# Expert weights kept on chip and addressed by a register, with the up products in split f16

## The chip, the cores and the metric

The kernel runs on one core of one Trainium2 chip. The metric is device time in microseconds of one launch. TensorE is called PE, ScalarE ACT, VectorE DVE, GpSimd POOL and SyncE SP.

## What is computed

32 images of 128 x 128 and 32 texts of 128 x 128 give 32 sequences of 192 tokens with 128 features. The part around the change is the last layer, cut here to what matters (xf is the normed sequence, K = 2 and 8 experts, F = 512):

```python
logits = xf @ router_w
gate_vals, idx = jax.lax.top_k(logits, K)
gates = jax.nn.softmax(gate_vals, axis=-1)
for e in range(E):
    h = jax.nn.relu(xf @ w1[e] + b1[e]) @ w2[e] + b2[e]
    y = _layernorm(xf + h, gamma[e], beta[e])
    w = jnp.sum(jnp.where(idx == e, gates, 0.0), axis=-1)
    out = out + w[:, None] * y
```

Ahead of it stand a noisy linear layer with a gate for the 64 patches of each image, the joining with the text, a norm, attention with 8 heads, a residual and a norm with weights, and one more norm. All is float32; the kernel already forms keys and queries from f16 halves.

## The kernel before

The work of every engine is written out by hand as one list of calls, with semaphores between engines.

**Attention stage.** The 32 sequences go in 16 pairs of 384 columns. PE embeds, forms keys, queries and values, scores (L828, L855), weighted values (L870, L873) and the projection. ACT copies and exponentiates (L599, L609, L633), DVE takes row maxima and norms, POOL shifts and scales rows (`shifted` L1616, `scale1` L1604 to L1610, which waits for DVE). DVE picks two experts for each token, and POOL sends each token's row to `sorted_d` in DRAM, to the place of its expert, by indirect DMA (`send`, L1653). SP issues nearly all loads. Among them is `pack(e)` (L442 to L450), which for each of the eight experts copies w1 and w2 (256 KB each), the small first bias, and gamma, beta and b2 (64 KB each, repeated over 128 rows) from their inputs into one DRAM tensor `pack_d`, six DMAs for each expert.

**Expert stage.** The sorted rows form 56 tiles: 47 of 256 rows and 9 of 128. A small `plan` on chip tells the expert of each tile. For a tile g SP does two things: `load(g)` (L475 to L483) reads the 256 token rows into `xs`, and `load_weights(g)` (L486 to L496) reads the expert from the plan into a register with `value_load` (L487), waits until the slot is free, and loads one expert's whole pack, 1413 floats a partition, into one of six slots `ws`. Four slots lie in the buffer of the stacked keys and queries (`stk`), two in one half of the exponentials' buffer (`pexs`).

PE works in steps (`step_b(nxt, cur, old)`, L933 to L966): the transposes of tile t+1 (L943), the up products of tile t (L953: four f32 matmuls with 256 columns, two records each in the trace), the down products of tile t-1 (L965: eight f32 matmuls with 128 columns, sixteen records). A tile of 128 rows has 128 columns in the up products, one transpose and half the down products. ACT's step (L663 to L681) copies the turned rows to SBUF (L668), makes four Relu passes (L675) and a square root (L681). DVE (L1418 to L1472) adds residual, bias and up result, norms, and gives the place of each row; POOL scatters the two halves of each result to `expert_d` (L1667). `b_xs`, `b_up`, `b_hid`, `b_dn` and `b_y` are the semaphores of turned rows, up products, hidden rows, down products and finished rows.

**Tail.** SP reads the results back (L530), ACT weights them (L722), DVE adds them (L1543, L1548), and SP stores them (L539, L542).

The lists of the stages overlap: PE's first ten expert steps stand among the last pieces of attention and routing of pairs 13 to 15.

## Time and profile before

| What | Value |
|---|---|
| Median of three runs | 606.3 us (605.55 to 612.3) |
| The profiled execution | 610.3 us |
| Its span from the first to the last instruction | 608.6 us |
| Mean granted TensorE clock | 0.936 of full speed |
| Moved by DMA | 101.61 MB, 167 GB/s on average |

The profiled execution is 1.7 us longer than its span and 4.0 us over the median. PE is the matmuls and PEld the weight loads, which overlap them; "issue" is idle time for which the profile shows no releaser, "remote" one that it puts down to no engine of the trace. Register operations are not counted as busy. Lines are those of the code above.

### The profile page before, as it was taken

Reading aid. Unit: us, or ns where it says so; the run is one execution under the profiler, and the core shown is the slowest. Engines: PE = TensorE matmul, PEld = TensorE weight load, DVE = VectorE, ACT = ScalarE, POOL = GpSimd, SP = SyncE. Lnnn points to the kernel's source line nnn. Section 1 sums busy time; section 2 is a strip of 40 time slices with the busy share of each in tenths; the row PEclk is TensorE's granted clock in tenths of the full one; section 3 lists DMA queues with packets and bytes.
Section 4 is the critical chain, followed back from the end, with each engine's and each line's share of the span. In section 5 each row is a group of like instructions: output and inputs, shape, how many; then the busy total and the mean of one; then the engine's idle time right before and its main releaser. Section 6 shows DMA issues by size and latency. Waiting matters only on the chain.

```text
span 608.6 us, 15887 instructions
## 1 busy us (share of the span) xinstructions
PE 505.8 (83%) x4764; PEld 402.4 (66%) x4764; DVE 445.2 (73%) x1768; ACT 343.2 (56%) x793; POOL 307.1 (50%) x447
## 2 busy tenths in 40 slices
PE   4899999988998799977667998798878998989800
PEld 3776676656666566755445797697767988989700
DVE  5875788966776589767656488478667778777797
ACT  4575667756566466755444555455354554655662
POOL 2530224577644645746726578555555555345430
PEclk9999999998999889989968999698999999999965
DMA  5266644361434216333103736566678989888599
GB/s 161 80 195 167 161 123 117 89 180 33 150 115 112 75 61 145 98 98 104 45 15 126 260 106 215 173 182 220 198 216 248 285 267 288 257 285 262 168 340 258
DMA packets 75078, 101.61 MB, mean 167 GB/s; under 512 B 10750, under 2 KB 58785, under 8 KB 74994
## 3 DMA queue, kind: packets, MB, share of 16 engines
q1 hardware_dynamic: 54114, 77.61, 43.4%
q0 software_dynamic: 6416, 12.93, 6.1%
q10 hardware_dynamic: 14464, 10.06, 5.5%
q8 instruction: 39, 0.64, 0.5%
q14 instruction: 45, 0.37, 0.2%
HBM read 74.40 MB, written 32.38 MB: 175 GB/s over the span
## 4 chain that ended last, share of the span: by engine, by line
PE 32%; issue 21%; DVE 15%; POOL 11%; another core or an unknown queue 6%; SPq 6%; ACT 5%; DMA 2%; ACTq 1%; POOLq 0%; DVEq 0%
PE sbk L953 7%; POOL sorted_d L1653 6%; PE avb L965 3%; PE mbk L965 3%; PE mbk L828 2%; PE avb L768 2%; PE sbk L855 2%; PE avb L870 2%; PE avb L873 1%; PE gen L768 1%; DVE pexs L1455 1%; DVE stat L1461 1%; POOL rs L1639 1%; PE gen L776 1%
## 5 line engine op out<-in xcount | busy, mean ns | idle before, releaser
L1156 DVE TENSOR_REDUCE mx<-mbk 128x4 f32<-128x768 f32 x96 | 91.1, 949 | 49.3 <-PE mbk L828 31.3
L1653 POOL DMA_INDIRECT sorted_d<-pay,slot x96 | 96.1, 1001 | 41.4 <-issue 26.5
L1667 POOL DMA_INDIRECT expert_d<-pexs,dest x70 | 70.4, 1006 | 65.0 <-DVE pexs L1455 46.1
L633 ACT ACTIVATE pexs<-sbk 128x768 f32<-128x768 f32 x96 | 77.5, 808 | 37.1 <-PE sbk L855 29.0
L953 PE MATMUL sbk<-pexs,stk 128*128 128x256 f32 (+1 forms) x304 | 71.4, 379 | 6.3 <-issue 4.4
L675 ACT ACTIVATE pexs<-sbk,stk 128x256 f32<-128x256 f32 (+1 forms) x152 | 59.5, 456 | 20.0 <-PE sbk L953 10.3
L953 PEld LDWEIGHTS sbk<-pexs,stk 128*128 128x128 f32 x304 | 54.1, 198 | 14.2 <-issue 8.3
L1667 POOL DMA_INDIRECT expert_d<-xT,dest x33 | 32.8, 995 | 34.2 <-DVE xT L1455 19.0
L668 ACT ACTIVATE pexs<-mbk 128x256 f32<-128x256 f32 (+1 forms) x55 | 19.7, 359 | 49.2 <-remote 38.5
L828 PE MATMUL mbk<-stk 48*64 48x192 f16 (+1 forms) x512 | 34.2, 258 | 14.8 <-DVE mx L1156 11.2
L855 PE MATMUL sbk<-stk 49*64 49x192 f16 (+1 forms) x512 | 34.8, 260 | 9.8 <-ACT pexs L633 5.7
L1616 POOL TENSOR_TENSOR kept<-h,lnb 128x384 f32<-128x384 f32 x16 | 16.0, 1000 | 50.9 <-DVE h L1131 50.7
L768 PE MATMUL avb<-ident 128*128 128x128 f32 x246 | 37.8, 296 | 0.0
L965 PEld LDWEIGHTS mbk<-stk,pexs 128*128 128x128 f32 x272 | 35.2, 200 | 2.5 <-issue 1.5
L965 PE MATMUL mbk<-stk,pexs 128*128 128x128 f32 x272 | 35.4, 283 | 1.4 <-issue 1.4
L870 PE MATMUL avb<-pexs,vxs 128*32 128x192 f32 x512 | 35.6, 352 | 0.5 <-issue 0.4
L873 PE MATMUL avb<-pexs,vxs 128*32 128x192 f32 x512 | 35.4, 342 | 0.6 <-issue 0.6
L965 PE MATMUL avb<-stk,pexs 128*128 128x128 f32 x288 | 35.3, 275 | 0.0
L768 PEld LDWEIGHTS avb<-ident 128*128 128x128 f32 x246 | 32.4, 201 | 4.4 <-issue 2.0
L965 PEld LDWEIGHTS avb<-stk,pexs 128*128 128x128 f32 x288 | 34.8, 192 | 0.8
L828 PEld LDWEIGHTS mbk<-stk 48*64 48x64 f16 (+1 forms) x512 | 12.3, 101 | 34.6 <-DVE mx L1156 17.2
L953 PE MATMUL sbk<-pexs 128*128 128x256 f32 (+1 forms) x144 | 31.8, 364 | 2.8 <-ACT pexs L675 2.8
(255 smaller groups left out, 1203.6 us busy)
## 6 DMA issues: line engine op xcount, KB each, us to landing
stk<-pack_d SPq DMA_DIRECT2D x38, 706.5 KB
pexs<-pack_d SPq DMA_DIRECT2D x18, 706.5 KB
stack_d<-kq ACTq DMA_DIRECT2D x48, 192.0 KB
stk<-stack_d SPq DMA_DIRECT2D x64, 144.0 KB
xn<-sorted_d SPq DMA_DIRECT2D x47, 132.0 KB
pack_d<-in_w SPq DMA_DIRECT2D x16, 256.0 KB
xin<-in_xp SPq DMA_DIRECT2D x16, 128.0 KB, 3.8
h<-in_txt SPq DMA_DIRECT2D x16, 128.0 KB, 3.6
```

Source lines behind the costliest of these rows:

```text
L633: act.activation(pex[p % 2][m][:, :, :], sbk[:, :, 0:COLS], ACT.Exp, scale=0.25).then_inc(a_pex, 1)
L675: act.activation(hid[cur % 2][:, c, 0:n], bank[4 + c // 2][:, (c % 2) * G:(c % 2) * G + n], ACT.Relu, bias=ws[cur % 6][:, AT_B1 + c:AT_B1 ...
L768: pe.matmul(place[:, COLS:512], ident[:, :], ident[:, :], start=True, stop=True)
L828: last = pe.matmul(dst, queries, keys, start=True, stop=True)
L855: last = pe.matmul(dst, keys, queries, start=True, stop=True)
L870: pe.matmul(dst, v[:, 1 + b, head, :], e[3 * g + 2 * pair][:, half, b * SEQ:(b + 1) * SEQ], start=True, stop=False)
L873: last = pe.matmul(dst, v[:, 3 * b, head, :], e[3 * g + 1][:, half, pair * SEQ:(pair + 1) * SEQ], start=False, stop=True)
L953: last = pe.matmul(bank[4 + c // 2][:, (c % 2) * G:(c % 2) * G + n], ws[cur % 6][:, c * P:(c + 1) * P], xsT[cur % 2][:, 0:n], start=True, ...
L965: last = pe.matmul(ok, hid[old % 2][:, c, k * P:(k + 1) * P], ws[old % 6][:, F + c * D:F + (c + 1) * D], start=(c == 0), stop=(c == FC - 1))
L1156: dve.tensor_reduce(dst, mbk[:, :, 0:COLS].rearrange("p h (c s) -> p h c s", c=2), AX.X, ALU.max).then_inc(d_mx, 1)
L1653: pool.indirect_dma_start(sorted_d[:, :], bass.IndirectOffsetOnAxis(ap=slot[p % 6][:, 2 * k + w:2 * k + w + 1], axis=0), pay[p % 6][:, k, ...
L1667: pool.indirect_dma_start(expert_d[:, :], bass.IndirectOffsetOnAxis(ap=dest[fin % DESTS][:, k:k + 1], axis=0), ye[fin % RESULTS][:, k, :], ...
```

## The change

The numbers for which only part of a tile's pack is loaded fall to 389 floats a partition (first bias, an id, gamma, beta and b2), and all six slots lie in one buffer. `pack(e)` loses its copies of w1 and w2 and has four DMAs.

w1 of all experts (2 MB) comes by one DMA early in the attention stage. It is split: POOL multiplies it by 256 (`enlarge`), ACT rounds it to f16 (`high_weights`), POOL subtracts that from it and rounds the rest to f16 (`low_weights`), each eight times with 128 x 512 elements. w2 of all experts (2 MB) comes as f32 by three DMAs (`second_weights`) into the key and query buffer, when the last score products of pairs 12 to 14 are done.

In an expert step PE reads the tile's expert into a register (`which`). The rows are turned two steps ahead; ACT makes the high half in f16 (`high`), PE takes it off the turned rows in PSUM by one f16 matmul with -1/256 times the identity (`drop_high`), and ACT makes the low half (`low`). The up products are, for each of four chunks, three f16 matmuls (high by high, low by high, high by low), whose weights are addressed by the register. The Relu pass scales by 1/65536. The down products stay eight f32 matmuls, with w2's rows addressed by the register. SP and POOL have the same calls per tile as before, save for waits.

Beside this, buffers of the plan and of the tail lie in other memory (`spare` goes, the second and third group of results lie in `hs`, `kqs`, `flat0`), semaphores of the setup are merged, and POOL fills one more 128 x 128 constant, `less`, at the start.

The core of the diff:

```diff
-AT_B1 = F + FC * D
+AT_B1 = 0
 AT_ID = AT_B1 + FC
 AT_LN = AT_ID + 1
-WROW = F + FC * D + FC + 1 + 3 * D
+WROW = FC + 1 + 3 * D
+SPLIT = 256.0
...
-        ws = [stk32[:, i * (4 * COLS):i * (4 * COLS) + WROW] for i in range(4)] + [flat0[:, i * WROW:(i + 1) * WROW] for i in range(2)]
+        ws = [flat0[:, i * WROW:(i + 1) * WROW] for i in range(6)]
+        w1s = sb("w1s", [P, NE, 2, F], F16)
+        w1f = flat1[:, 0:NE * F].rearrange("p (e f) -> p e f", e=NE)
+        w2s = stk32[:, 0:NE * FC * D].rearrange("p (e c d) -> p e c d", e=NE, c=FC)
...
-        xsT = [room(2048 + 256 * i, (G,)) for i in range(2)]
+        xsT = [room(2048 + 256 * i, (G,)).bitcast(F16).rearrange("p (a t) -> p a t", a=2) for i in range(2)]
...
-        spare = sb("spare", [P, 2 * GROUP * TILES * D])
-        y1 = [group_of(stk32, 3072), group_of(vxf, 0), group_of(spare, 0), group_of(stk32, 0)]
-        y2 = [group_of(stk32, 4608), group_of(vxf, 1536), group_of(spare, 1536), group_of(stk32, 1536)]
-        w_in, wa_in, small_made = sem("w_in"), sem("wa_in"), sem("small_made")
+        hsf = hs[:, :, :, :].rearrange("p i t d -> p (i t d)")
+        kqf = kqs[:, :, :, :].rearrange("p i j t -> p (i j t)").bitcast(F32)
+        assert 6 * WROW <= 2560
+        y1 = [group_of(stk32, 4608), group_of(vxf, 0), group_of(hsf, 0), group_of(stk32, 0)]
+        y2 = [group_of(flat0, 2560), group_of(vxf, 1536), group_of(kqf, 0), group_of(stk32, 1536)]
...
             def pack(e):
-                sp.wait_ge(small_made, 1)
-                for at, src in ((0, a["w1"][e]), (AT_B1, small[:, e, :]), (AT_LN, a["gamma"][e:e + 1, :].to_broadcast([P, D])),
+                sp.wait_ge(setup, 3)
+                for at, src in ((AT_B1, small[:, e, :]), (AT_LN, a["gamma"][e:e + 1, :].to_broadcast([P, D])),
                                 (AT_LN + D, a["beta"][e:e + 1, :].to_broadcast([P, D])),
                                 (AT_LN + 2 * D, a["b2"][e:e + 1, :].to_broadcast([P, D]))):
                     sp.dma_start(pack_d[e, :, at:at + src.shape[1]], src).then_inc(pack_out, 16)
-                sp.dma_start(pack_d[e, :, F:F + FC * D].rearrange("p (c d) -> p c d", c=FC),
-                             a["w2"][e].rearrange("(c p) d -> p c d", p=P)).then_inc(pack_out, 16)
-            PACKS = 6 * NE
+            PACKS = 4 * NE
+            def first_weights():
+                sp.dma_start(w1f, a["w1"].rearrange("e p f -> p e f")).then_inc(w12_in, 16)
+            def second_weights(i):
+                after(sp, pe_s, PAIRS - 4 + i, MERGED)
+                lo, hi = 3 * i, min(3 * i + 3, NE)
+                sp.dma_start(w2s[:, lo:hi, :, :].rearrange("p e c d -> p (e c) d"),
+                             a["w2"][lo:hi].rearrange("e (c p) d -> p (e c) d", p=P)).then_inc(w12_in, 16)
...
+            ldx(0); ldt(0); load_weights_a(); ldx(1); ldt(1); ldx(2); ldt(2); ldx(3); ldt(3); ldx(4); ldt(4); first_weights(); ldx(5)
...
             def load_weights(g):
                 e = sp.value_load(plan[0:1, 1, slot_of(g):slot_of(g) + 1], min_val=0, max_val=NE - 1)
-                if g < 4:
-                    after(sp, pe_s, PAIRS - 4 + g, MERGED)
-                elif g < 6:
+                if g < 6:
                     after(sp, pe_av, PAIRS - 2, 2)
                 after(sp, b_y, g - 6)
-                after(sp, b_dn, g - 6)
                 sp.dma_start(ws[g % 6], pack_d[bass.ds(e, 1), :, :].rearrange("a p f -> (a p) f")).then_inc(ws_in[g % 6], 16)
-            load_weights(0)
-            load_weights(1)
+            second_weights(0)
+            second_weights(1)
             for p in range(EARLY_PAIRS - 6, EARLY_PAIRS):
                 after_dma(sp, sent, p, 6)
             load(0)
             load(1)
+            second_weights(2)
+            load_weights(0)
+            load_weights(1)
             for g in range(2, 6):
...
+            def high_weights(e):
+                act.wait_ge(w1_made, e + 1)
+                act.activation(w1s[:, e, 0, :], w1f[:, e, :], ACT.Copy).then_inc(act_fills, 1)
...
+                if p == 1 and m == 0:
+                    act.wait_ge(w1_made, 2 * NE)
...
-            def step_b(nxt, cur):
-                if 0 <= nxt < GRID:
-                    act.wait_ge(b_xt, nxt + 1)
-                    after(act, b_up, nxt - 2, 2)
-                    n = chunks(nxt) * P
-                    act.activation(xsT[nxt % 2][:, 0:n], (bank[6] if nxt else gen_of("b0", 0))[:, 0:n], ACT.Copy).then_inc(b_xs, 1)
-                if 0 <= cur < GRID:
-                    n = chunks(cur) * P
+            def turned(t):
+                return (bank[6] if t else gen_of("b0", 0))[:, 0:chunks(t) * P]
+            def high(t):
+                if t < GRID:
+                    act.wait_ge(b_xt, t + 1)
+                    after(act, b_up, t - 2, 2)
+                    act.activation(xsT[t % 2][:, 0, 0:chunks(t) * P], turned(t), ACT.Copy, scale=SPLIT).then_inc(b_hi, 1)
+            def low(t):
+                if t < GRID:
+                    act.wait_ge(b_ng, t + 1)
+                    act.activation(xsT[t % 2][:, 1, 0:chunks(t) * P], turned(t), ACT.Copy, scale=SPLIT).then_inc(b_xs, 1)
+            def hidden(t):
+                if t < GRID:
+                    n = chunks(t) * P
                     for c in range(FC):
-                        act.wait_ge(b_up, cur * 2 + c // 2 + 1)
+                        act.wait_ge(b_up, t * 2 + c // 2 + 1)
                         if c == 0:
-                            after(act, b_dn, cur - 2)
-                        act.activation(hid[cur % 2][:, c, 0:n], bank[4 + c // 2][:, (c % 2) * G:(c % 2) * G + n],
-                                       ACT.Relu, bias=ws[cur % 6][:, AT_B1 + c:AT_B1 + c + 1]).then_inc(b_hid, 1)
-                if ROOT <= cur - 2 < GRID:
-                    old = cur - 2
-                    after(act, b_rs, old - 2)
-                    act.wait_ge(b_mv, old + 1)
-                    act.activation(sd4[old % 2][:, 0:chunks(old)], mv4[old % 2][:, 0:chunks(old), 1], ACT.Sqrt, bias=epsf[:, 0:1]).then_inc(b_sd, 1)
+                            after(act, b_dn, t - 2)
+                            after_dma(act, ws_in, t)
+                        act.activation(hid[t % 2][:, c, 0:n], bank[4 + c // 2][:, (c % 2) * G:(c % 2) * G + n], ACT.Relu,
+                                       bias=ws[t % 6][:, AT_B1 + c:AT_B1 + c + 1], scale=1.0 / (SPLIT * SPLIT)).then_inc(b_hid, 1)
+            def root(t):
+                if ROOT <= t < GRID:
+                    after(act, b_rs, t - 2)
+                    act.wait_ge(b_mv, t + 1)
+                    act.activation(sd4[t % 2][:, 0:chunks(t)], mv4[t % 2][:, 0:chunks(t), 1], ACT.Sqrt, bias=epsf[:, 0:1]).then_inc(b_sd, 1)
+            def step_b(t):
+                low(t + 1)
+                hidden(t)
+                high(t + 2)
+                root(t - 2)
...
+            xt(3); high_weights(0); high_weights(1); hi(3); vcopy(2); vcopy(3); high_weights(2); lo(3); xt(4); xnorm(5); hi(4); mxt(0); xt(5); gexp(6); lo(4); gexp(7)
+            high_weights(3); high_weights(4); hi(5); high_weights(5); lo(5); soft(0, 0); soft(0, 1); soft(0, 2); soft(0, 3); high_weights(6); high_weights(7); context(0, 0); soft(0, 4); soft(0, 5)
...
-            def step_b(nxt, cur, old):
-                if 0 <= nxt < GRID:
-                    after_dma(pe, xs_in, nxt)
-                    if nxt == 0:
+            expert = {}
+            def which(t):
+                if t < GRID:
+                    pe.wait_ge(plan_made, 1 if t < EARLY else 3)
+                    expert[t] = pe.value_load(plan[0:1, 1, slot_of(t):slot_of(t) + 1], min_val=0, max_val=NE - 1)
+            def turned(t):
+                return bank[6] if t else gen_of("b0", 0)
+            def turn(t):
+                if t < GRID:
+                    after_dma(pe, xs_in, t)
+                    if t == 0:
                         freed(gen_at, "b0", 0)
-                    if nxt == 1:
+                    if t == 1:
                         after(pe, d_cn, PAIRS - 1)
-                    after(pe, b_xs, nxt - 1)
-                    turned = bank[6] if nxt else gen_of("b0", 0)
-                    for k in range(chunks(nxt)):
-                        last = pe.transpose(turned[:, k * P:(k + 1) * P], xs[nxt % 6][:, k, 0:D], ident[:, :])
+                    after(pe, b_xs, t - 1)
+                    for k in range(chunks(t)):
+                        last = pe.matmul(turned(t)[:, k * P:(k + 1) * P], xs[t % 6][:, k, 0:D], ident[:, :], start=(k == 0), stop=True,
+                                         is_transpose=True, skip_group_check=True)
                     last.then_inc(b_xt, 1)
-                if 0 <= cur < GRID:
-                    after_dma(pe, ws_in, cur)
-                    pe.wait_ge(b_xs, cur + 1)
-                    if cur == 0:
-                        after(pe, a_pex, PAIRS - 1, MERGED)
-                    n = chunks(cur) * P
+            def drop_high(t):
+                if t < GRID:
+                    n = chunks(t) * P
+                    pe.wait_ge(b_hi, t + 1)
+                    pe.matmul(turned(t)[:, 0:n], less[:, :], xsT[t % 2][:, 0, 0:n], start=False, stop=True,
+                              skip_group_check=True).then_inc(b_ng, 1)
+            def up(t):
+                if t < GRID:
+                    n = chunks(t) * P
                     for c in range(FC):
-                        after(pe, b_hid, cur - 1, FC, c + 2 - c % 2)
-                        last = pe.matmul(bank[4 + c // 2][:, (c % 2) * G:(c % 2) * G + n],
-                                         ws[cur % 6][:, c * P:(c + 1) * P], xsT[cur % 2][:, 0:n], start=True, stop=True)
+                        if c == 0:
+                            pe.wait_ge(b_xs, t + 1)
+                        after(pe, b_hid, t - 1, FC, c + 2 - c % 2)
+                        if t == 0 and c == 0:
+                            pe.wait_ge(w1_made, 2 * NE)
+                            after(pe, a_pex, PAIRS - 1, MERGED)
+                        for i, (x, w) in enumerate(((0, 0), (1, 0), (0, 1))):
+                            rows = w1s[:, bass.ds(expert[t], 1), w, c * P:(c + 1) * P].rearrange("p e f -> p (e f)")
+                            last = pe.matmul(bank[4 + c // 2][:, (c % 2) * G:(c % 2) * G + n], rows, xsT[t % 2][:, x, 0:n],
+                                             start=(i == 0), stop=(i == 2))
                         if c % 2:
                             last.then_inc(b_up, 1)
-                if 0 <= old < GRID:
-                    if old == 0:
+            def down(t):
+                if 0 <= t < GRID:
+                    pe.wait_ge(b_hid, t * FC + FC)
+                    after(pe, b_z, t - 2)
+                    if t == 0:
+                        pe.wait_ge(w12_in, 16 * 4)
                         after(pe, a_cx, PAIRS - 1, 2)
-                    pe.wait_ge(b_hid, old * FC + FC)
-                    after(pe, b_z, old - 2)
-                    for k in range(chunks(old)):
-                        ok = bank[3 + 4 * (old % 2)][:, k * D:(k + 1) * D]
+                    for k in range(chunks(t)):
+                        ok = bank[3 + 4 * (t % 2)][:, k * D:(k + 1) * D]
                         for c in range(FC):
-                            last = pe.matmul(ok, hid[old % 2][:, c, k * P:(k + 1) * P],
-                                             ws[old % 6][:, F + c * D:F + (c + 1) * D], start=(c == 0), stop=(c == FC - 1))
+                            rows = w2s[:, bass.ds(expert[t], 1), c, :].rearrange("p e d -> p (e d)")
+                            last = pe.matmul(ok, hid[t % 2][:, c, k * P:(k + 1) * P], rows, start=(c == 0), stop=(c == FC - 1))
                     last.then_inc(b_dn, 1)
+            def step_b(t):
+                drop_high(t + 1)
+                up(t)
+                which(t + 1)
+                turn(t + 2)
+                down(t - 1)
...
+            which(0); turn(0); turn_x2(13); drop_high(0); turn_context(15); up(0); which(1); route(13); turn_c(15)
+            turn(1); down(0); project(15); drop_high(1); count(13); turn(2); drop_high(2); up(1); which(2); turn(3)
+            step_b(2); turn_x2(14); step_b(3); route(14); step_b(4); count(14); step_b(5); step_b(6); step_b(7)
+            turn_x2(15); step_b(8); route(15); step_b(9); count(15)
...
+            def enlarge(e):
+                if e == 0:
+                    pool.wait_ge(w12_in, 16)
+                pool.tensor_scalar(w1f[:, e, :], w1f[:, e, :], SPLIT, None, ALU.mult).then_inc(w1_made, 1)
+            def low_weights(e):
+                pool.wait_ge(act_fills, 4 + e + 1)
+                pool.wait_ge(w1_made, e + 1)
+                pool.tensor_tensor(w1s[:, e, 1, :], w1f[:, e, :], w1s[:, e, 0, :], ALU.subtract).then_inc(w1_made, 1)
...
+            scale1(1); shifted(2); scale1(2); shifted(3); scale1(3); shifted(4); scale1(4); enlarge(0); enlarge(1); enlarge(2); shifted(5); scale1(5)
+            enlarge(3); enlarge(4); enlarge(5); enlarge(6); enlarge(7); low_weights(0); low_weights(1); low_weights(2)
+            low_weights(3); low_weights(4); low_weights(5); shifted(6); scale1(6); low_weights(6); low_weights(7); shifted(7); scale1(7); shifted(8); scale1(8); shifted(9); scale1(9); scale2(0)
```

## Rows read from the trace of the kernel before

**Rows 1.** the page: busy time of the engines, and the chain that ended last

```profile
PE 505.8 (83%) x4764; PEld 402.4 (66%) x4764; DVE 445.2 (73%) x1768; ACT 343.2 (56%) x793; POOL 307.1 (50%) x447
...
PE 32%; issue 21%; DVE 15%; POOL 11%; another core or an unknown queue 6%; SPq 6%; ACT 5%; DMA 2%; ACTq 1%; POOLq 0%; DVEq 0%
```

**Rows 2.** windows, core 0: us, busy and count by engine, granted clock, DMA share, GB/s

```profile
250.00:345.40 95.40, 74.56 (x909) 51.95 (x908) 59.10 (x248) 49.43 (x96) 55.09 (x77) 0.89 0.31 93
345.40:578.60 233.20, 208.87 (x1432) 192.84 (x1430) 174.06 (x802) 123.62 (x347) 126.25 (x134) 0.97 0.73 228
578.60:608.60 30.00, 0.14 (x2) 0.00 (x0) 25.60 (x84) 14.27 (x47) 6.06 (x6) 0.55 0.93 299
```

**Rows 3.** timeline of PE, full tiles: start us, us, engine, line, operation, tiles, count

```profile
370.00 1.89 PE L953 MATMUL sbk<-pexs,stk 128*128 128x256 f32 x8
371.73 1.95 PE L965 MATMUL mbk<-pexs 128*128 128x128 f32 x16
373.51 0.38 PE L943 MATMUL mbk<-ident,xn 128*128 128x128 f32 x2
373.73 0.60 PE L953 MATMUL sbk<-pexs,stk 128*128 128x256 f32 x2
```

**Rows 4.** the same view, a half tile and a full one in turn

```profile
486.38 1.06 PE L953 MATMUL sbk<-pexs,stk 128*128 128x128 f32 x8
...
492.00 1.89 PE L953 MATMUL sbk<-pexs,stk 128*128 128x256 f32 x8
```

**Rows 5.** waits of the expert stage (total us, times, longest us), one stall of PE

```profile
ACT pexs L668 <- remote: 38.5, 12, 5.2
...
PEld mbk L943 <- DMA xn<-sorted_d: 5.4, 4, 2.5
...
383.05 1.50 PE L953 MATMUL sbk<-pexs,stk 128*128 128x256 f32 x4 [3.81 <-issue]
```

**Rows 6.** timeline of PE: f16 matmuls of 384 columns, and three small bf16 ones

```profile
78.15 0.49 PE L801 MATMUL sbk<-kq,minus 128*128 128x384 f16 x2
...
352.81 0.17 PE L929 MATMUL gen<-oh,before 128*128 128x24 bf16 x1
352.84 0.22 PE L924 MATMUL gen<-oh,onesb 128*128 128x16 bf16 x3
```

**Rows 7.** chain of waits at 461 us, SyncE: start us, us, what (plan read, address, move, DMA)

```profile
461.10 0.26 SPq L487
...
461.71 0.04 SPq L496
...
461.80 0.03 SPq L496
...
461.86 0.34 SPq L496
```

**Rows 8.** timeline of DVE, one round of tiles; groups of the stage by line

```profile
370.94 0.61 DVE L1425 SCALAR_TENSOR_TENSOR pexs<-pexs,mv,stk 128x128 f32<-128x128 f32 x2
...
373.90 0.35 DVE L1425 SCALAR_TENSOR_TENSOR pexs<-pexs,mv 128x128 f32<-128x128 f32 x1
...
L1667 POOL DMA_INDIRECT expert_d<-pexs,dest x66 | 66.4, 1006 | 61.5 <-DVE pexs L1455 44.2 <-issue 16.5 <-DVE dest L1436 0.6
...
L675 ACT ACTIVATE pexs<-sbk,stk 128x256 f32<-128x256 f32 x128 | 52.5, 472 | 17.0 <-PE sbk L953 7.5 <-remote 5.5 <-issue 3.4
```

**Rows 9.** DMA issues of the page: tensors, queue, operation, count, KB each

```profile
stk<-pack_d SPq DMA_DIRECT2D x38, 706.5 KB
...
pack_d<-in_w SPq DMA_DIRECT2D x16, 256.0 KB
```

**Rows 10.** attention stage: windows row, one POOL wait, and line L599

```profile
47.40:97.00 49.60, 48.00 (x552) 32.68 (x549) 36.76 (x82) 31.59 (x60) 9.16 (x20) 1.00 0.57 148
...
64.18 1.00 POOL L1616 TENSOR_TENSOR kept<-h,lnb 128x384 f32<-128x384 f32 x1 [16.74 <-DVE h L1131]
...
L599 ACT ACTIVATE kq<-sbk x16: 788/810/811, 26.6 to 279.4; 128x768 f16<-128x768 f32 x16
```

85 lines of the change are left out of this document (42 added, 43 removed).

## The prediction, made before the changed kernel had run

> **What bounds the kernel now.** I read the page first. TensorE is the busiest engine (505.8 us, 83% of a 608.6 us span) and the largest named share of the chain that ended last, 32%, but "issue", DVE and POOL share the rest [rows 1], so the stages have to be read one by one. The windows say that up to 345.4 us the attention stage runs, then 233.2 us of expert tiles in which PE is busy 208.87 us, DVE 174.06, ACT 123.62 and POOL 126.25 at a DMA share of 0.73, and that in the last 30 us PE does nothing and DMA is 0.93 busy [rows 2]. The change works in the middle one, and in the attention stage it adds work.
>
> Inside an expert step the PE timeline shows what is paid. A full tile (256 rows) starts 3.73 us after the one before (370.00 to 373.73): two transposes, eight up records in 1.73 us (370.00 to 371.73), sixteen down records in 1.78 (371.73 to 373.51) and 0.22 for the next transposes, with no gap [rows 3]. A half tile and a full one together take 5.62 us (486.38 to 492.00) [rows 4]. With 47 full and 9 half tiles, 38 lone full ones and 9 such pairs make 38 x 3.73 + 9 x 5.62 = 192 us of the 233; the other 41 are the attention leftovers, slow starts and stalls. The waits list names them: ACT's copy of the turned rows waits 38.5 us for "remote", PEld waits 5.4 us for row loads; and before 383.05 us one tile stands for 3.81 us in "issue" [rows 5]. What a stall is worth is thus not known from its name, but the array is the limit of every clean tile.
>
> **The up products.** One f32 matmul of 256 columns (two records) becomes three f16 ones. The f16 pair L801 has 384 columns: two in 0.49 us. The small bf16 ones of 16 to 24 columns show 0.17 us from start to end with hardly any streaming, so 0.49 - 0.17 = 0.32 us is the streaming of two, 0.16 each; 256 columns are 0.107 us. Twelve of them: 1.29 us for 1.73. One more, drop_high, 0.107; transposes 0.22 and down 1.78 as they are. Array time of a full tile: 0.22 + 0.11 + 1.29 + 1.78 = 3.40, say 3.43 with the joints; 0.30 saved. A pair of half and full: 0.33 + 0.16 + 1.94 + 2.67 = 5.1 for 5.62 [rows 3, 4, 6].
>
> **The register.** This is the unknown. PE now reads the tile's expert from the plan and its 12 up weights and 8 down rows are addressed by it. No row shows a TensorE instruction like that. The nearest are SyncE's, which does the same for each weight load. On the chain at 461 us: the plan read starts at 461.10, the address computation at 461.71, a move at 461.80, the DMA at 461.86 [rows 7]. So a read costs 0.61 us, one address 0.09 (0.04 of it the operation), a move 0.06. Plain instructions cost the PE sequencer next to nothing: three bf16 matmuls with weights in 0.22 us where one takes 0.17, 0.03 apart [rows 6]. Sequencer time of a full tile: 0.61 + 20 x (0.09 + 0.03) + 11 other pairs x 0.03 = 3.3 us, just under the array's 3.43: hidden, if the sequencer can run ahead. For a half tile: 0.61 + 16 x 0.12 + 6 x 0.03 = 2.7; a pair of half and full is 6.0, over the array's 5.1 and over the 5.62 of before. The lower end is nothing (address computed beside the array, 3.43); the upper has all 28 addressed records (the 16 down records one by one) at address, move and issue, 0.18: 0.61 + 5.0 = 5.7 us a tile. I take the 0.12, because a matmul needs the address and no descriptor, and 20, one for each matmul written. The Trainium skill (TensorE: Matmul & The Clock Gate, "Wait — 56ns, not 53.3ns?") says that a MATMUL decoded by the sequencer's own code costs about 62 ns. The 0.03 spacing shows that plain ones here don't pay it; whether addressed ones do, no row shows; by that rule the full tile would be 3.3 + 20 x 0.062 = 4.5 us, estimated from that page.
>
> Stage: 38 x (3.43 - 3.73) = -11.4; 9 pairs x (6.0 - 5.62) = +3.4, of which the sequencer's lead from full tiles (0.13 each) takes half: +1.7. Sum -9.7.
>
> **The other engines in a step.** They must fit below 3.43. DVE's chain repeats from 370.94 to 373.90, 2.96 us [rows 8]: it fits by 0.5. ACT: four Relus and now two copies of the same size for one, at most 6 x 0.472 = 2.8 us, and a small square root. POOL has two scatters of 1.006 us and idles 16.5 us of the stage before 66 of them for their issue, 0.25 each: 2.5 us a tile. In the early tiles sends of the same kind come on top, which makes some of these tiles POOL's [rows 8]. Transposes are issued two steps ahead and ACT halves them in two passes with a PE pass between (low waits for drop_high); its place at the step's head gives it a step of cover. If it is late, each tile pays a pass, 0.47 us.
>
> **Loads.** The per-tile load falls from 706.5 KB to 199 [rows 9]: 56 x 0.507 = 28.4 MB less, in a stage of 228 GB/s [rows 2]. PE was no longer waiting for weights but for rows [rows 5]; these 5.4 us stand behind the same queue. About half of it goes: -3. It could be all the stalls in part (-12) or none.
>
> **The attention stage.** DVE leads POOL there: POOL waits 16.74 us at 64.18 for h, and is busy 9.16 us of the 49.6 from 47.4 on [rows 10]. The eight enlargements and eight subtractions, 128x512, by the tensor operation of 128x384 at 1.0 us are at most 1.33 each: 21 us. They fill the 16.7 us window and spill 4 to 5 into those behind, all with idle time: 0, at worst one pair late by 5. ACT gets 8 copies, 0.5 to 0.8 each by the 0.81 of 768 columns [rows 10]: 5 us in a stretch in which it is busy 31.59 of 49.6 and PE 48.0; the score chain waits at times for ACT, so I charge half, +2.5. Soft(1,0) waits for the last halves; behind it stand the whole score rows of pair 1. The 2 MB load, 7 us at the tail's 299 GB/s [rows 2], stands ahead of the inputs of pairs 5 and later, which are loaded many pairs ahead. Against this 16 DMA to DMA copies of 256 KB, 8 MB in and out, and their issues on SP are gone [rows 9]; SP only feeds buffers there: -0.5. Sum +2, ends -1 and +8. The second weights (three loads, 2 MB) come at the end of that stage, at a DMA share of 0.31 [rows 2], ahead of row loads 0 and 1 on SP: +1. The tail reads the same bytes: 0.
>
> **Sum.** -9.7 - 3 + 2 + 1 = -9.7 us against the profiled execution, which took 610.3 (span 608.6 and 1.7 around it), 4.0 above the median of 606.3. So 596.5 on the scale of the medians. About 1%, 6 us, is what a measurement of this kernel can tell from no change.
>
> **Rivals.**
> (A) The sequencer becomes the bound. Every matmul with a register costs more than (3.73 - 0.61 - 0.33)/20 = 0.14 us: from there on the expert step is slower than before. At address, move and issue (0.18, 20 times) a full tile is 4.5 and a half one 3.7: 38 x 0.8 + 9 x 2.6 = +54, so 660; with 28 addressed records at 0.12 it is 4.1 and 3.1: 38 x 0.33 + 9 x 1.5 = +26, so 630. I take 635. For it: SP's rows. Against it: the read and the addresses need nothing of the tile before, and can run while the array works. The 4.5 us by the Trainium skill's figure for sequencer decoding falls at its upper end.
> (B) PE's time is not the limit on average. 41 us of stage don't come from the array, and a faster one waits longer for DVE, POOL's scatters and the freezes. Then only part of the 9.7 comes, and the attention stage's additions eat it: 604. For it: "remote" and "issue" waits that no PE row explains. Against it: runs of clean tiles at 3.73.
> (C) The loads were behind the stalls. With 28 MB less, SP's queue and the row loads are on time and a third of the 41 us goes: -14 beside the 9.7: 583. For it: the step of 378 us. Against it: "remote" stalls lie also where the DMA share is low.
>
> **Chances.** Forecast 0.35 (596.5, own range 590 to 601); A 0.28; B 0.17; C 0.17; that the early splitting delays pair 1 by more than 8 us 0.03. Range 578 to 640: it leaves out the upper half of A. Faster by over 1% (under 600.2): 0.28 + 0.17 + 0.02 = 0.47; within 1%: 0.07 + 0.15 = 0.22; slower: 0.31.
>
> **What would show it.** Full tiles starting 3.4 us apart in the PE timeline, up 1.3 of it; no "issue" gaps between the addressed matmuls. A: up records 0.13 or more apart instead of 0.107, down pairs over 0.112, PE waiting for its own queue. B: 3.4 us bursts and larger waits of ACT and DVE. C: fewer "remote" waits. DMA share of the stage near 0.4; the first expert tile at 345 to 349 us, later if the splitting hurts. The prediction is wrong if a clean full tile takes over 3.6 us.

## The result, and the profile after

The changed kernel takes 641.17 us in the median (640.78 to 644.29, four runs) against 605.92 for the kernel before, a ratio of 1.0615 with a 95% interval of 1.0553 to 1.0677. It is slower by some 35 us. The forecast was 596.5 us, the range ended at 640, and rival A, on the slower side, was priced at 635. The profiled execution has a span of 639.1 us. Some executions of a kernel run slower than its others at a lower granted clock; the ratios leave these out, and no stage times are given from them.

The page of the changed kernel, its busy times and the chain that ended last:

```profile
PE 508.0 (79%) x5044; PEld 393.1 (62%) x5044; DVE 448.5 (70%) x1768; ACT 360.8 (56%) x857; POOL 329.2 (52%) x465
...
PE 46%; ACT 15%; another core or an unknown queue 11%; issue 10%; DVE 8%; DMA 4%; ACTq 2%; SPq 2%; POOL 1%; DVEq 0%; POOLq 0%
```

Beside [rows 1], ACT has grown from 5% to 15% of the chain, with only 17.6 us more work. The windows of the changed kernel (columns as in [rows 2]) say where the time went:

```profile
250.00:346.10 96.10, 80.50 (x939) 55.17 (x939) 62.63 (x259) 52.10 (x102) 58.62 (x83) 0.89 0.33 94
346.10:607.70 261.60, 210.45 (x1710) 183.77 (x1709) 176.14 (x802) 136.26 (x401) 126.07 (x133) 0.94 0.36 100
607.70:639.10 31.40, 0.00 (x0) 0.00 (x0) 26.00 (x84) 15.03 (x49) 6.25 (x6) 0.53 0.93 297
```

The first up product starts at 346.10 us, where it started at 345.39: the split of w1 on POOL and ACT and the early load cost the attention stage 0.7 us. The tail is 1.4 us longer. The expert stage grew from 233.2 to 261.6 us, 28.4 of the 30.5 us, although its DMA share fell from 0.73 to 0.36 and its rate from 228 to 100 GB/s.

A clean tile is what was forecast. The timeline of PE (columns as in [rows 3]):

```profile
493.57 1.47 PE L1024 MATMUL sbk<-pexs,w1s 128*128 128x256 f16 x12
494.88 0.38 PE L999 MATMUL mbk<-ident,xn 128*128 128x128 f32 x2
495.10 1.98 PE L1041 MATMUL avb<-stk,pexs 128*128 x16
496.92 0.27 PE L1008 MATMUL mbk<-pexs,less 128*128 128x256 f16 x1
497.03 1.47 PE L1024 MATMUL sbk<-pexs,w1s 128*128 128x256 f16 x12
498.42 0.30 PE L999 MATMUL mbk<-ident,xn 128*128 128x128 f32 x1
```

The timeline of ACT in the same tile:

```profile
494.53 1.56 ACT L712 ACTIVATE pexs<-sbk,pexs 128x256 f32<-128x256 f32 x4
495.95 0.41 ACT L695 ACTIVATE pexs<-mbk 128x256 f16<-128x256 f32 x1
...
497.23 0.38 ACT L701 ACTIVATE pexs<-mbk 128x256 f16<-128x256 f32 x1 [0.68 <-PE mbk L1008]
```

From 493.57 to 497.03 is 3.46 us (the shortest are 3.42) for 3.73 in [rows 3]; the twelve up products take 1.31 us to the transposes, 0.109 each. But the same rows show how thin the cover is. ACT ends the high half (L695) at 496.36, and drop_high (L1008), which waits for it, starts at 496.92: 0.56 us. ACT can begin the four Relus that stand ahead of it only when the first half of the up products is done, some 0.82 us after their start (five times 0.109 and the sixth one's 0.27). Here the Relus start 0.14 us after that (494.53), so a message that comes more than some 0.7 us late delays the whole chain. The next hand-overs are as close: the low half (L701) ends at 497.61, and the next transposes, which write to the bank that it reads, start at 498.42.

How large such delays are is seen at 555 us, in a timeline of ACT, POOL and PE (rows of weight loads left out):

```profile
554.84 1.17 PE L1024 MATMUL sbk<-pexs,w1s 128*128 128x128 f16 x12
...
555.10 0.97 POOL L1763 DMA_INDIRECT expert_d<-pexs,dest  x1 [0.30 <-issue]
555.55 0.62 ACT L712 ACTIVATE pexs<-sbk,pexs 128x128 f32<-128x128 f32 x2 [0.20 <-issue]
...
556.63 0.97 POOL L1763 DMA_INDIRECT expert_d<-xT,dest  x1 [0.56 <-issue]
...
557.90 0.97 POOL L1763 DMA_INDIRECT expert_d<-xT,dest  x1 [0.30 <-issue]
559.55 0.62 ACT L712 ACTIVATE pexs<-sbk,pexs 128x128 f32<-128x128 f32 x2 [3.38 <-remote]
560.07 0.38 ACT L695 ACTIVATE pexs<-mbk 128x256 f16<-128x256 f32 x1
...
560.51 0.28 PE L1008 MATMUL mbk<-pexs,less 128*128 128x256 f16 x1 [1.64 <-ACT pexs L695]
```

The twelve matmuls ended at 556.01. The update of their first half released the first two Relus at once, but the last two start only at 559.55, after a run of POOL's indirect DMAs. "remote" is the profile's word for it. Then ACT writes the next high half, and PE, which has long been ready, waits for that. I counted for both kernels how often a Relu, with ACT idle and its matmuls ended, starts more than 0.25 us late: of the 112 messages (two a tile), 11 in the kernel before, 14.3 us together, and 19 in the changed one, 38.0 us. All 30 fall in an indirect DMA or within 0.5 us after one. Since indirect DMAs fill much of this stage, many punctual messages fall there as well: 11 of 84 such messages are late in the kernel before and 0 of the other 28, 19 of 52 and 0 of the other 60 in the changed one. Counted the same way over all nine kernels that have the indirect scatters, 200 of 644 messages near an indirect DMA are late, and 4 of the 364 others.

The stall of 3.81 us in [rows 5], which the view calls "issue", is one of them: PE waits there for Relus that start late. The timeline of ACT in the kernel before, for matmuls that ended at 375.62:

```profile
382.16 0.84 ACT L675 ACTIVATE pexs<-sbk,stk 128x256 f32<-128x256 f32 x2 [4.17 <-remote]
```

The waits of the changed kernel's expert stage (total us, times, longest us) show who pays:

```profile
ACT pexs L701 <- PE mbk L1008: 39.2, 36, 2.9
ACT pexs L712 <- remote: 33.2, 12, 4.0
...
PEld mbk L1008 <- ACT pexs L695: 28.6, 16, 5.2
PEld mbk L999 <- issue: 27.5, 35, 4.5
```

The third line has no counterpart in the kernel before: 28.6 us of PE waiting for the high half. The fourth is PE standing ahead of the transposes; in the last 32 tiles it comes to 11.2 us in 23 waits of at most 0.8 us, and the experiments come back to these. A second price follows: after a stop the granted clock is at its lower level, 1.2 GHz. The mean clock of the stage is 0.94 (0.97 in [rows 2]), which makes 2 x 0.06 x 261.6 = 31 us at half speed against 14. One stop and the step after it, in the timelines of PE and ACT:

```profile
442.22 1.47 PE L1024 MATMUL sbk<-pexs,w1s 128*128 128x256 f16 x12
445.47 0.84 ACT L712 ACTIVATE pexs<-sbk,pexs 128x256 f32<-128x256 f32 x2 [2.67 <-remote]
449.81 0.84 ACT L712 ACTIVATE pexs<-sbk,pexs 128x256 f32<-128x256 f32 x2 [3.50 <-remote]
450.98 0.40 PE L1008 MATMUL mbk<-pexs,less 128*128 128x256 f16 x1 [4.98 <-ACT pexs L695]
451.18 2.75 PE L1024 MATMUL sbk<-pexs,w1s 128*128 128x256 f16 x12
```

The matmuls ended at 443.69, and their last two Relus start 6.1 us later, behind five indirect DMAs that run from 442.48 to 448.79 with pauses of 0.3 us. Twelve up products then take 2.75 us for 1.47. The windows of this stretch show the stop and the clock (PE busy 0.03 of 5.00 us, then a granted clock of 0.50):

```profile
446.00:451.00 5.00, 0.03 (x1) 0.03 (x1) 1.54 (x9) 1.50 (x5) 2.18 (x3) 0.80 0.34 93
451.00:454.00 3.00, 3.00 (x15) 2.22 (x16) 2.71 (x11) 1.35 (x5) 0.99 (x1) 0.50 0.36 87
```

So PE is busy for 210.45 us, more than the 208.87 of [rows 2], with less to do.

### The profile page after: what moved, and what is told of

It reads as the page before. It is cut to its first block, busy times and chain, and to the rows that moved or that the text cites. A ratio compares the mean times of both kernels' runs of the same rounds, so it can differ in the third digit from the quotient of the medians.

```text
span 639.1 us, 17319 instructions
## 1 busy us (share of the span) xinstructions
PE 508.0 (79%) x5044; PEld 393.1 (62%) x5044; DVE 448.5 (70%) x1768; ACT 360.8 (56%) x857; POOL 329.2 (52%) x465
## 4 chain that ended last, share of the span: by engine, by line
PE 46%; ACT 15%; another core or an unknown queue 11%; issue 10%; DVE 8%; DMA 4%; ACTq 2%; SPq 2%; POOL 1%; DVEq 0%; POOLq 0%
PE sbk L1024 6%; PE avb L1041 5%; ACT pexs L712 4%; PE mbk L1041 4%; PE sbk L900 4%; PE avb L918 3%; PE avb L915 3%; PE mbk L873 3%; PE sbk L840 2%; ACT pexs L657 2%; PE avb L813 2%; PE mbk L999 2%; PE gen L813 2%; DVE mx L1238 2%
## 5 line engine op out<-in xcount | busy, mean ns | idle before, releaser
L712 ACT ACTIVATE pexs<-sbk,pexs 128x256 f32<-128x256 f32 (+1 forms) x224 | 85.1, 457 | 52.6 <-remote 33.2
L1024 PE MATMUL sbk<-pexs,w1s 128*128 128x256 f16 (+1 forms) x672 | 82.2, 272 | 0.1
L1024 PEld LDWEIGHTS sbk<-pexs,w1s 128*128 x672 | 62.2, 100 | 11.1 <-issue 0.2
L1041 PE MATMUL avb<-stk,pexs 128*128 x424 | 59.7, 299 | 0.0
L1041 PEld LDWEIGHTS avb<-stk,pexs 128*128 128x128 f32 x424 | 55.9, 212 | 1.4 <-issue 0.2
L1041 PE MATMUL mbk<-stk,pexs 128*128 x400 | 51.7, 282 | 0.0
L701 ACT ACTIVATE pexs<-mbk 128x256 f16<-128x256 f32 (+1 forms) x55 | 20.1, 365 | 55.1 <-PE mbk L1008 39.2
L813 PE MATMUL avb<-ident 128*128 128x128 f32 x246 | 38.5, 300 | 0.0
L999 PE MATMUL mbk<-ident,xn 128*128 128x128 f32 x101 | 22.3, 297 | 19.9 <-ACT pexs L701 14.5
L1008 PE MATMUL mbk<-pexs,less 128*128 128x256 f16 (+1 forms) x55 | 15.1, 275 | 28.0 <-ACT pexs L695 25.6
L1507 DVE SCALAR_TENSOR_TENSOR pexs<-pexs,mv 128x128 f32<-128x128 f32 x103 | 32.8, 355 | 1.5
## 6 DMA issues: line engine op xcount, KB each, us to landing
xn<-sorted_d SPq DMA_DIRECT2D x47, 132.0 KB
```

The costliest lines, as they stand in the source:

```text
L712: act.activation(hid[t % 2][:, c, 0:n], bank[4 + c // 2][:, (c % 2) * G:(c % 2) * G + n], ACT.Relu, bias=ws[t % 6][:, AT_B1 + c:AT_B1 + c ...
L813: pe.matmul(place[:, COLS:512], ident[:, :], ident[:, :], start=True, stop=True)
L1024: last = pe.matmul(bank[4 + c // 2][:, (c % 2) * G:(c % 2) * G + n], rows, xsT[t % 2][:, x, 0:n], start=(i == 0), stop=(i == 2))
L1041: last = pe.matmul(ok, hid[t % 2][:, c, k * P:(k + 1) * P], rows, start=(c == 0), stop=(c == FC - 1))
```

## Experiments

Three ideas were to be told apart. Theory S: the messages between engines are held up around POOL's indirect DMAs in both kernels, and the changed step has a PE-ACT round trip with too little cover to bear it. Theory R: the register holds PE's sequencer. And the loads: they could be behind the stalls or not. Times of one line were taken on one chip in turn with the kernel before (606 to 614 us, by the chip), so ratios are compared. The last two columns are the expert stage from the start of the first up product to that of the last tile's in the profiled execution, in us, split at the 24th tile: tiles 0 to 22, and the 32 after them. They come from one execution each, which can lie some us off its kernel's median (deep 636.1 for 644.7, deep_rows8 618.6 for 624.2), so a difference of a few us in them says nothing without the ratios. A dash means that none is given.

| Kernel | us | ratio to before | tiles 0-22 | last 32 |
|---|---|---|---|---|
| before | 605.9 | 1 | 113.1 | 114.9 |
| changed | 641.2 | 1.0615 (1.0553-1.0677) | 131.9 | 124.3 |
| split_static | 630.7 | 1.0275 (1.0207-1.0343) | - | - |
| no_hop | 620.5 | 1.0138 (1.0103-1.0172) | 116.1 | 115.4 |
| static_no_hop | 614.8 | 1.0100 (1.0013-1.0186) | - | - |
| plain_before | 580.0 | 0.9457 (0.9422-0.9492) | 94.0 | 103.6 |
| plain_after | 598.8 | 0.9797 (0.9746-0.9847) | 102.7 | 107.8 |
| plain_static | 583.7 | 0.9574 (0.9462-0.9686) | 101.4 | 99.5 |
| plain_no_hop | 575.0 | 0.9487 (0.9418-0.9557) | 96.7 | 97.3 |
| plain_static_no_hop | 573.6 | 0.9428 (0.9346-0.9509) | 94.4 | 95.5 |
| late_which | 649.6 | 1.0528 (1.0435-1.0622) | 132.0 | 130.9 |
| deep | 644.7 | 1.0491 (1.0429-1.0552) | 131.9 | 124.8 |
| plain_deep | 615.8 | 0.9941 (0.9878-1.0004) | - | - |
| deep_rows8 | 624.2 | 1.0295 (1.0209-1.0380) | 125.8 | 113.6 |
| plain_deep_rows8 | 577.8 | 0.9522 (0.9472-0.9573) | 98.9 | 96.7 |
| w2_only | 611.8 | 1.0059 (0.9957-1.0161) | - | - |

**The register taken out (split_static).**

```diff
-                    expert[t] = pe.value_load(plan[0:1, 1, slot_of(t):slot_of(t) + 1], min_val=0, max_val=NE - 1)
+                    expert[t] = 0
...
-                            rows = w1s[:, bass.ds(expert[t], 1), w, c * P:(c + 1) * P].rearrange("p e f -> p (e f)")
+                            rows = w1s[:, 0:1, w, c * P:(c + 1) * P].rearrange("p e f -> p (e f)")
...
-                            rows = w2s[:, bass.ds(expert[t], 1), c, :].rearrange("p e d -> p (e d)")
+                            rows = w2s[:, 0:1, c, :].rearrange("p e d -> p (e d)")
```

> The changed kernel (641.2 us) with the register taken out: no plan read on TensorE, every tile uses the weights of expert 0 at a fixed address (the choice of the expert is left out; same instructions otherwise). Theory S (short cover: PE's semaphore updates are held up around POOL's indirect DMAs in both kernels, and the changed step needs PE-ACT round trips with only about 0.65 us of cover): the round trips are all still there, so 630 to 641 us. Theory R (the register: plan read and address operations hold PE's sequencer, so it can't run ahead): 605 to 615 us. If both act: between.

1.0275: between the two. The gain is more than S alone allows (630.7 us lies in its range only because this chip runs the kernel before in 612.6 us). Some 45% of the loss stays with no register in the kernel.

**The round trip taken out (no_hop).**

```diff
-                    act.activation(xsT[t % 2][:, 0, 0:chunks(t) * P], turned(t), ACT.Copy, scale=SPLIT).then_inc(b_hi, 1)
+                    act.activation(xsT[t % 2][:, 0, 0:chunks(t) * P], turned(t), ACT.Copy, scale=SPLIT)
+                    act.activation(xsT[t % 2][:, 1, 0:chunks(t) * P], turned(t), ACT.Copy, scale=SPLIT).then_inc(b_xs, 1)
...
-                    act.wait_ge(b_ng, t + 1)
-                    act.activation(xsT[t % 2][:, 1, 0:chunks(t) * P], turned(t), ACT.Copy, scale=SPLIT).then_inc(b_xs, 1)
...
-                    pe.wait_ge(b_hi, t + 1)
-                    pe.matmul(turned(t)[:, 0:n], less[:, :], xsT[t % 2][:, 0, 0:n], start=False, stop=True,
-                              skip_group_check=True).then_inc(b_ng, 1)
```

> The changed kernel with the extra round trip taken out: drop_high is gone (one matmul of 0.11 us a tile), ACT writes high and low halves one after the other, two steps ahead (the low half is then no remainder: the subtraction is left out). Register, three products and ACT's count of passes stay. Theory S: the cover of each step is back to over 2 us, the 3.43 us of a clean tile hold: 595 to 608 us. Theory R: 630 to 641 us.

1.0138, 620.5 us: outside the 595 to 608 expected, but four fifths of the loss are gone, with one matmul of 0.11 us a tile taken away and the number of ACT's passes unchanged. By the count above ACT's Relus start late 30 times here, 54.1 us together, more than in the changed kernel: the delays are there, and most of them are covered.

**Both taken out (static_no_hop).**

> Changed kernel without the round trip (no drop_high, both halves copied at once) and without the register (expert 0 for all tiles). The indirect scatters stay. If hop and register are separate costs that add up (20 and 30 us of about 37 are more than the whole, so they overlap): about 600 us, 0.98 of before, which leaves the array's saving of 0.3 us a tile. If the register cost only showed because the hop left no cover (theory S): same as no_hop, 1.01 of before.

The edits of the two together: 1.0100 (1.0013 to 1.0186). This is what S said, the same as no_hop. The two gains (3.4 and 4.8 points) don't add up (5.2 together); without the round trip the register costs some 0.4 points, less than the error.

**The scatters as plain DMAs (plain_before, plain_after).**

```diff
...
-                        pool.indirect_dma_start(expert_d[:, :], bass.IndirectOffsetOnAxis(ap=dest[fin % DESTS][:, k:k + 1], axis=0),
-                                                ye[fin % RESULTS][:, k, :], None, bounds_check=2 * TOKENS - 1, oob_is_err=False
-                                                ).then_inc(ye_out[fin % RESULTS], 16)
...
+                sp.wait_ge(b_y, t + 1)
+                sp.dma_start(expert_d[at:at + n * P, :].rearrange("(c p) d -> p c d", c=n), ye[t % RESULTS][:, 0:n, :]
+                             ).then_inc(ye_out[t % RESULTS], 16)
```

> The changed kernel with the expert stage's scatters on POOL replaced by plain DMAs of the same bytes on SP's queue to fixed rows (the placing of the results is left out). Theory S: no indirect DMA, no hold-up; hardly any update comes over 0.3 us late after tile 21, tiles start 3.43 us apart there, 600 to 615 us, nearly all of the 35 us gone against the same edit of the kernel before. Theory R: the tiles of the late part stay at 3.8 to 4.2 us on average, 630 or more.

> The kernel before with the same edit of its scatters. Theory S: it gains less than the changed kernel, 5 to 20 us (590 to 600), since its step covers most hold-ups; afterwards both stand within 10 us of each other. Theory R: the distance between the two edited kernels stays at 30 us or more.

Neither theory has it all. The kernel before gains 33 us, more than the 5 to 20 of S; the changed one gains 8.2 points of ratio, some 50 us. So 35 us of loss become 19, between the 10 of S and the 30 of R. The edit takes away three things at once, the indirect form, POOL as the issuer and the scattered places, and it adds waits on SyncE; which of them counts isn't told apart. No late Relu is left in plain_before, one (0.3 us) in plain_after, and the "remote" waits of ACT, 38.5 us in [rows 5], are 1.0 us in the list of plain_before and none in that of plain_after. The kernel before now runs its late tiles at its clean period, one after the other, at full clock:

```profile
442.60:546.20 103.60, 103.16 (x752) 98.04 (x751) 84.33 (x380) 65.96 (x192) 0.00 (x0) 1.00 0.93 294
```

PE is busy 103.16 of 103.60 us at a DMA share of 0.93 and 294 GB/s: the loads that the change takes away hid entirely behind it, and most of the stalls of [rows 5] went with the scatters. What is left of the changed kernel's loss shows in its timeline:

```profile
483.05 0.23 PE L1020 MATMUL mbk<-pexs,less 128*128 128x128 f16 x1 [0.17 <-ACT pexs L707]
483.25 1.48 PE L1036 MATMUL sbk<-pexs,w1s 128*128 128x256 f16 x12
485.02 0.41 PE L1011 MATMUL mbk<-ident,xn 128*128 128x128 f32 x2 [0.30 <-issue]
```

Eight address operations 0.124 us apart and a plan read of 0.65 us are 1.6 us of the sequencer beside 1.31 us of up products. Where PE has just waited and its sequencer has no lead, the transposes come 0.3 us late, then ACT's high half, then drop_high. With the register out (plain_static, a tile of the same kind) they follow after 1.31 us:

```profile
477.13 1.47 PE L1036 MATMUL sbk<-pexs,w1s 128*128 128x256 f16 x12
478.44 0.38 PE L1011 MATMUL mbk<-ident,xn 128*128 128x128 f32 x2
```

**The same square with plain scatters (plain_static, plain_no_hop, plain_static_no_hop).**

> Changed kernel with plain scatters and without the register. Against plain_after (598.8, itself 19 above plain_before): theory R' (the plan read stands between the up products and the transposes, and a step that starts on time has 1.86 us of sequencer work for 1.31 us of array work there): full tiles 3.43, pairs of half and full under 5.8, 575 to 585. Theory S' (hop without cover even with no hold-up): no gain, 595 to 600.

> Changed kernel with plain scatters and without the round trip; the register stays. Theory R': the pattern of 3.3 and 3.9 us stays, 590 to 597. Theory S': clean 3.3 us tiles, 575 to 582.

> Changed kernel with plain scatters, no round trip, no register: what the array's saving is worth with everything else taken away. By the steps 3.32 us a full tile against 3.73 in plain_before, so 56 tiles give 15 to 20 us: 562 to 570, 0.97 to 0.98 of plain_before (580.0), unless DVE (3.3 us a tile) is the next bound.

The pattern is the same as with the scatters, without their noise: 0.9797 with both, 0.9574 without the register, 0.9487 without the round trip, 0.9428 without either. plain_static came out as R' said and plain_no_hop as S' said. Either edit alone takes away most of the late loss (8.3 and 10.5 us of the 12.3 between 107.8 and 95.5), so in these tiles neither is the cause by itself: each costs mainly where the other stands. Again the register costs 2 points while the round trip stands and about half a point without it, within the error. In tiles 0 to 9 it is otherwise. They take 50.4 us in plain_after and 50.7 in plain_static, but 42.8 in plain_no_hop, 41.3 in plain_static_no_hop and 41.0 in plain_before: there the round trip alone costs 8 to 9 us. With everything taken away the late tiles take 95.5 us for 103.6, so the array's saving is 8 us there; in tiles 0 to 22, among the leftovers of attention, it is nothing (94.4 and 94.0). The whole kernel then is no faster than plain_before beyond the error (0.9428 and 0.9457), less than the 562 to 570 us expected.

**The plan read moved (late_which).**

```diff
-                which(t + 1)
                 turn(t + 2)
                 down(t - 1)
+                which(t + 1)
```

> The changed kernel with one call moved: TensorE reads the next tile's expert behind the down products instead of between the up products and the transposes. Nothing is left out. If the 0.3 us gaps ahead of the transposes are the register's part (0.65 us of reading on a sequencer that has no lead there), most of what split_static gained (1.0615 to 1.0275 of before) comes: 1.03 to 1.045. If it is the count of register operations and not their place: 1.055 to 1.065.

1.0528 (1.0435 to 1.0622): its interval overlaps that of the changed kernel, and it lies between the two expected ranges. The place of the read alone is not the whole of the 3 points. It did what it was meant to: in the last 32 tiles PE's "issue" waits ahead of the transposes fall from 11.2 us (23 times) to 3.8 (5 times). But PE's waits for the high half stay (9.8 us in the changed kernel, 16.5 in the execution profiled here). The move was not tried with plain scatters.

**The round trip given cover (deep, plain_deep).**

```diff
                 low(t + 1)
                 hidden(t)
-                high(t + 2)
+                high(t + (3 if t >= DEEP else 2))
...
                 up(t)
+                turn(t + 3)
+                down(t - 1)
                 which(t + 1)
-                turn(t + 2)
-                down(t - 1)
+                drop_high(t + 2)
```

(Against the changed kernel, with DEEP = 14. The plan read of late_which is in it: `which` stands behind `down`.)

> late_which, and from tile 14 on the rows are turned three steps ahead into one of three PSUM banks, with four split buffers: drop_high comes at the end of a step, low at the start of the next one, each hand-over then has over 2 us of cover instead of 0.65. Nothing is left out. Theory S (cover): the late part of the stage comes down to that of static_no_hop (114.9 us for the last 32 tiles, 124.3 in the changed kernel), total 1.02 to 1.035 of before; the first 14 tiles stay slow. If the hop costs by its work (one matmul, one wait) and not by its missing cover: no gain over late_which.

> deep with plain scatters (placing of the results left out). Theory S: clean full tiles at 3.42 us and pairs of half and full at 5.6 or less in the last 32 tiles, which then take 99 to 101 us against 107.8 in plain_after and 103.6 in plain_before; total 0.955 to 0.965 of before.

Neither shows what S forecast: 1.0491, which by the number is the "no gain over late_which" of the other theory, and 0.9941, slower than plain_after (0.9797). The wait list of deep from 417 us on gives the reason; a new wait had taken the place of the old one:

```profile
PEld mbk L1004 <- DMA xn<-sorted_d: 16.0, 11, 3.2
PEld gen L1004 <- DMA xn<-sorted_d: 15.4, 14, 3.1
```

Turning three steps ahead asks for a row load that itself waits for one of six row buffers. These two runs tell nothing about S.

**And row buffers to go with it (deep_rows8, plain_deep_rows8).**

```diff
-                after(sp, b_z, g - 6)
-                after(sp, b_dest, g - 6)
+                after(sp, b_z, g - 8)
+                after(sp, b_dest, g - 8)
...
-                load(g)
+                if g + 2 < GRID:
+                    load(g + 2)
                 load_weights(g)
```

> deep with a ring of eight row buffers instead of six and the row loads issued two tiles ahead of the loads of the norm rows. Nothing is left out. In deep PE waited some 33 us for row loads late in the stage, because turning three steps ahead asks for rows that wait for a buffer. Theory S (missing cover): these waits go, the last 32 tiles take about 115 us as in static_no_hop and no_hop (124.8 in deep), total 1.01 to 1.03 of before. If the round trip costs by its work: 124 stays, 1.045 or more.

> The same with plain scatters (placing left out). Theory S: last 32 tiles 99 to 101 us (107.8 in plain_after, 120.7 in plain_deep, 103.6 in plain_before), no waits for rows. Otherwise 107 or more.

Both go the way S says, the second further than it said. deep_rows8 leaves nothing out, has the register, the matmul drop_high and all its waits, and its last 32 tiles take 113.6 us (124.3 in the changed kernel, 114.9 before; this execution is 5.6 us below its median); the ratio falls from 1.0615 to 1.0295, and the intervals of the two, and of deep_rows8 and late_which, do not meet. With plain scatters 107.8 become 96.7, and 0.9797 becomes 0.9522, about where taking the round trip out had brought it. So the round trip cost by its missing cover and not by its work. The edit has three parts, the later plan read, the deeper order and the earlier row loads. The last of them had nothing to win by itself: in its last 32 tiles PE waits for no row load in the changed kernel, and for one in plain_after:

```profile
PEld mbk L1011 <- DMA xn<-sorted_d: 0.4, 1, 0.4
```

With the scatters the read's place alone left the late tiles at 130.9. With plain scatters, how much of the 11 us belongs to it and how much to the deeper order is not told apart.

The timeline of plain_deep_rows8, two full tiles, shows no gap with all of it in place:

```profile
460.13 1.47 PE L1047 MATMUL sbk<-pexs,w1s 128*128 128x256 f16 x12
461.44 0.27 PE L1022 MATMUL mbk<-ident,xn 128*128 128x128 f32 x1
461.55 1.95 PE L1064 MATMUL avb<-stk,pexs 128*128 x16
463.33 0.27 PE L1031 MATMUL gen<-pexs,less 128*128 128x256 f16 x1
463.44 1.47 PE L1047 MATMUL sbk<-pexs,w1s 128*128 128x256 f16 x12
```

(The first of them has one transpose, since the tile three ahead is a half one: 3.31 us.) Most of what deep_rows8 still loses lies in tiles 0 to 9, where the old order stands: 61.0 us for 51.1 before.

**Half of the change (w2_only).** w1 in the pack again, four f32 up products, one copy on ACT, w2 on chip:

```diff
-WROW = FC + 1 + 3 * D
+WROW = F + FC + 1 + 3 * D
...
+                        last = pe.matmul(bank[4 + c // 2][:, (c % 2) * G:(c % 2) * G + n], ws[t % 6][:, c * P:(c + 1) * P],
+                                         xsT[t % 2][:, 0:n], start=True, stop=True)
```

> One half of the change alone: w2 stays on chip and is addressed by the register (the plan is read behind the down products), w1 is loaded per tile (450.5 KB instead of 706.5) and the up products are the four f32 matmuls of before; no split, no round trip; rows turned two steps ahead. Nothing is left out. Theory S: no hand-over without cover, so the step is as robust as that of before, and the loads of before weren't what it waited for: 0.99 to 1.015 of before. If the register itself costs (12 or more operations a tile and the read): 1.02 to 1.035. If loads held before up: 0.97 to 0.985.

1.0059 (0.9957 to 1.0161), no difference that can be told. The resident w2 with the plan read and four address operations a tile cost no more than the error (1.6%) where no round trip leans on the sequencer, and 14 MB less of loads bring nothing that shows.

None of the seven kernels of the experiments that keep the indirect scatters is faster than the kernel before beyond the error.

## Why the prediction was wrong

**What held.** The array: 3.42 to 3.46 us for a clean full tile, forecast 3.43, with 0.109 us for an up product (0.107). A half tile and a full one together take 5.2 to 5.3 us in plain_deep_rows8, where PE hardly waits; the forecast had 5.1 for the array and 6.0 for the sequencer, so its +1.7 for these pairs was a term that isn't there. The attention stage: +0.7 us at the first up product, forecast +2 and +1. That the sequencer is not the bound of a full tile; my 3.3 us for it were too much. The instructions of the up and down lines on PE's weight queue (count, ns shortest, median and longest, first and last start):

```profile
L1024 PEldq FUSED_REGOPS  x448: 46/46/46, 346.0 to 602.3; - x150
...
L1041 PEldq FUSED_REGOPS  x224: 46/46/51, 348.8 to 605.3; - x112
```

These are 8 and 4 operations a tile (448 and 224 over 56 tiles), since matmuls with the same rows share an address, 12 and not 20; 0.124 us apart as assumed. With the read (0.65, from 0.61 on SyncE) and the other instructions a tile is some 2.5 us.

The Trainium skill's figure of about 62 ns for a MATMUL that the sequencer's code decodes (TensorE: Matmul & The Clock Gate, "Wait — 56ns, not 53.3ns?") does not show here. Down records with a register-held address stand 0.112 us apart in the trace, as the plain ones of [rows 3]; a cost of 0.06 could hide in that. But clean tiles keep 3.43 us, where by the prediction's estimate it would have made 4.5.

**What failed.** The step is "its place at the step's head gives it a step of cover". Only low stands at the head, and even its result is needed in the same step, 0.8 us later, by the next transposes. The high half had 0.56 us of cover in the clean tile above, because high comes behind four Relus that wait for the up products of the same step. The sum put the round trip at nothing. The sentence behind it, "If it is late, each tile pays a pass, 0.47 us", would have made 56 x 0.47 = 26 us, near the 28.4 that the stage grew by, but it was in no sum and no rival, and the loss doesn't come as 0.47 in each tile: it comes in stops of up to 5 us in some of them. I had summed the engines' work (ACT 2.8 us of 3.43) and not followed the chain PE, Relus, high, drop_high, low, transposes through two steps. In the kernel before, the copy of the turned rows stands at the head of ACT's step and is needed a step later. Given cover again, the late tiles fall to 113.6 us.

A second term fell with it, the register at nothing: "hidden, if the sequencer can run ahead". After a wait it is not ahead, and the read placed between the up products and the transposes then delays these by 0.3 us (plain_after). Taking the register out gives back 3.4 points, taking the round trip out 4.8, both 5.2.

With these two went the reading of the stalls. I took the 41 us beyond the clean tiles for a stock that the change would, if anything, reduce, "-3" by smaller loads, and rival C a third of it. plain_before shows what most of it was: the scatters cost 33 us, by hold-ups that a step covers or does not. The changed kernel covers less, so the same cause cost it about 50. Rival C is refuted: with 28 MB less there are more late Relus and not fewer, w2_only gains nothing by 14 MB less, and plain_before has clean tiles at 294 GB/s. Rival B, that a faster array waits longer for the others, had the direction right; even with no round trip (no_hop) the late tiles took 115.4 us, as before.

**Rival A** was near the time (635) by luck and wrong in its mechanism. No clean tile is sequencer-bound at 4.1 to 4.5 us. The register costs 2 to 3 points, but only beside the round trip without cover. late_which took most of the waits ahead of the transposes away, yet gained at most a part of these points; why so little with the scatters in place stays open.

## What to carry to other kernels

When a step is moved to an earlier or later place, write down each hand-over between engines with its cover: when the result is there in a clean step, and when it is needed. The busy time of the engines says nothing of it, and a chain of three hand-overs with half a microsecond each turns hiccups into stops, and stops into a slow clock. Find out first what the stalls of the old kernel are (here by leaving out the one suspected instruction), for a change that adds round trips multiplies them. And giving a step more lead needs buffers for whatever now has to come earlier.
